# Windowed attention on one core: rotated queries and keys moved to whole heads, scores as products over 64 rows

## The reference, cut to what matters

```python
DEPTH, HEADS, DIM_HEAD, WINDOW = 6, 16, 64, 32      # x: (4, 512, 128)
q, k, v = (heads of x @ Wqkv)
q, k = l2norm(q) * qs, l2norm(k) * ksc
q = q * cos * scale + rotate_half(q) * sin * scale  # rotate_half: (-x2, x1)
k = k * cos / scale + rotate_half(k) * sin / scale
# each block of 32 queries sees its own 32 keys and the 32 before
attn = softmax(q_blk @ k_2blk.T * 8 where not masked)
x = x + (attn @ v_2blk) @ Wo, then x = x + gated FFN(layernorm(x))
```

## Time and profile before

| | |
|---|---|
| median of 3 runs | 2510.15 us (2502.93 to 2514.1) |
| the profiled execution | span 2515.4 us; no other time stands with it |
| instructions | 122,084, of them 53,677 MATMUL and as many LDWEIGHTS |
| transformer stage | from about 120 to 1845 us |
| DMA | 204.62 MB, mean 81 GB/s |

### The profile page before, as it was taken

How to read it: one execution, slowest core, us unless ns; L and a number is a source line. 1 busy time by engine, 2 the same in 40 slices (tenths; PEclk the granted TensorE clock), 3 DMA queues, 4 the chain that set the end, 5 groups by cost and what they waited for, 6 DMA issues and landing times.

```text
span 2515.4 us, 122084 instructions
## 1 busy us (share of the span) xinstructions
PE 2362.9 (94%) x53677; PEld 1738.9 (69%) x53677; DVE 1744.7 (69%) x3537; ACT 1598.6 (64%) x5036; POOL 1463.1 (58%) x1408
## 2 busy tenths in 40 slices
PE   9958999999999999999999999999878999999967
PEld 8836777777777777777777777777645666666657
DVE  4477888888878888878787888887335555555534
ACT  3226777777777787777777877777625444545422
POOL 1166667656666667666666677665117656566307
PEclk9979999999999999999999999999979999999978
DMA  4013333333333334333333343333216222222136
GB/s 91 15 33 86 85 78 96 95 80 85 93 88 94 81 83 103 92 83 81 88 95 85 79 97 82 84 92 84 57 22 185 48 48 48 48 48 48 30 95 250
DMA packets 230210, 204.62 MB, mean 81 GB/s; under 512 B 133687, under 2 KB 155464, under 8 KB 229552
## 3 DMA queue, kind: packets, MB, share of 16 engines
q1 hardware_dynamic: 225296, 190.91, 30.6%
q0 software_dynamic: 2208, 5.58, 0.6%
q10 hardware_dynamic: 2176, 0.33, 0.1%
HBM read 86.05 MB, written 15.70 MB: 40 GB/s over the span
## 4 chain that ended last, share of the span: by engine, by line
PE 72%; DVE 17%; issue 4%; SPq 2%; ACT 2%; DMA 1%; POOL 1%; POOLq 0%; ACTq 0%; DVEq 0%
PE psum L1208 8%; PE psum L1226 6%; PE psum L1955 5%; PE psum L1234 5%; PE psum L1109 5%; PE psum L1934 5%; PE psum L1940 4%; PE psum L1111 4%; PE psum L1110 3%; DVE kT L1443 3%; PE psum L1989 3%; PE psum L1979 3%; DVE rotated L1418 3%; PE psum L1185 2%; PE psum L1216 2%
## 5 line engine op out<-in xcount | busy, mean ns | idle before, releaser
L1354 ACT ACTIVATE p<-p,stat 128x64 f32<-128x64 f32 x1536 | 512.5, 336 | 40.1 <-DVE stat L1490 38.0
L1573 POOL TENSOR_TENSOR p<-p,inverse 128x512 f32<-128x512 f32 x192 | 200.2, 1043 | 465.9 <-DVE inverse L1493 464.9
L1208 PE MATMUL psum<-kT,qT 32*32 32x64 f32 x24576 | 306.7, 223 | 30.3 <-issue 29.1
L2088 DVE TENSOR_REDUCE largest<-psum 128x1 f32<-128x512 f32 x256 | 165.0, 686 | 228.0 <-PE psum L1940 228.0
L1208 PEld LDWEIGHTS psum<-kT,qT 32*32 32x32 f32 x24576 | 264.0, 103 | 82.2 <-issue 81.1
L1354 ACT ACTIVATION_READ_ACCUMULATOR p<-p,stat 128x1 f32 x1536 | 288.6, 188 | 0.0
L1418 DVE SCALAR_TENSOR_TENSOR rotated<-psum,scales,rotary 128x512 f32<-128x512 f32 x384 | 271.1, 742 | 24.3 <-ACT sq L1290 24.2
L1552 POOL TENSOR_TENSOR sq<-sq 128x512 f32<-128x512 f32 x192 | 245.1, 1276 | 42.4 <-ACT sq L1290 42.1
L1290 ACT ACTIVATE sq<-psum 128x512 f32<-128x512 f32 x384 | 212.8, 581 | 63.3 <-PE psum L1139 45.9
L1226 PEld LDWEIGHTS psum<-pT,v_win 64*64 64x64 f32 x12288 | 197.3, 135 | 47.6 <-issue 40.6
L1109 PE MATMUL psum<-xs,wqkv_high 128*128 128x512 f32 x384 | 204.9, 534 | 24.3 <-DVE rotated L1418 24.3
(11 more groups left out here) (352 smaller groups left out, 5448.6 us busy)
## 6 DMA issues: line engine op xcount, KB each, us to landing
v_win<-v_tok SPq DMA_DIRECT2D x576, 128.0 KB
rnorm_wide<-rnorms SPq DMA_DIRECT2D x384, 64.0 KB
v_win<-v_tok SPq DMA_DIRECT2D x336, 64.0 KB
q_rows<-q_rows_all SPq DMA_DIRECT2D x32, 512.0 KB, 4.6
tile_weights<-expert_table SPq DMA_DIRECT2D x23, 512.0 KB, 6.1
wqkv<-L_ffn_Wqkv SPq DMA_DIRECT2D x96, 64.0 KB, 2.4
rel_values<-sq SPq DMA_DIRECT2D x60, 64.0 KB, 2.2
wo<-L_ffn_Wo SPq DMA_DIRECT2D x48, 64.0 KB
```

Of the source, the lines that this page charges most:

```text
L1208: last = PE.e.matmul(psum[WIN * blk:WIN * (blk + 1), f, out], q[rows, g, half, tok:tok + WIN], k[rows, g, half, tok:tok + 2 * WIN], start= ...
L1354: last = A.e.activation(p, p, ACT.Exp, bias=t.stat[:, h, 2 * g + f:2 * g + f + 1], accum_out=t.sum[:, h, g, f:f + 1])
L1573: G.e.tensor_tensor(p, p, t.inv[:, h, :, :].unsqueeze(3).to_broadcast([P, GROUPS_TF, 2, 2 * WIN]), ALU.mult).then_inc(*t.p_scaled.by(m))
```

## The change

Each rotated half is written to one of three stage buffers. When GpSimd has finished it, SP moves it with two DMAs (`relay`): heads now lie whole in 64 partitions (`[half::2]`: the halves' features interleaved, in the same manner for queries and keys), two heads side by side. A score is then one product over 64 rows. A part's even and odd heads go to slots that change places for blocks 2 and 3 (`swapped`), odd heads' values are projected from tokens with each tile's 64-token halves exchanged (`x_swapped`, by ScalarE and GpSimd), and so ScalarE's copy of the values already is the window of the odd blocks; DMAs make that of the even ones alone. The mixing reads its two halves of 64 queries from two places. Norms are spread by 2 DMAs a group instead of 4. Several steps change rounds.

```diff
-VALUE_FIRST, WINDOWS_AT = 29, 31
+VALUE_FIRST, WINDOWS_AT, SWAP_AT = 33, 37, 28
-SQUARES_LAG, SUM_LAG, MADE_LAG = 2, 4, 3
-NORM_AT = {"root0": 17, "out": 15, "root1": 33, "turn": 39, "copy": 39}
-SPREAD_AT = (16, 18, 19, 24)
-SCALE_AT = (24, 28, 29, 32)
+SQUARES_LAG, SUM_LAG, MADE_LAG, RELAY_LAG = 2, 4, 3, 4
+NORM_AT = {"root0": 17, "out": 19, "root1": 33, "turn": 39, "copy": 39}
+SPREAD_AT = (20, 21, 25, 28)
+SCALE_AT = (24, 27, 28, 32)
+STAGES = 3
-SPLIT_AT = {2: 13, 3: 31, 0: 39, 1: 40, 4: 56, 5: 59}
+SPLIT_AT = {2: 13, 3: 31, 0: 39, 1: 40, 4: 60, 5: 62}
...
+def swapped(f, blk):
+    return f if blk < TPB // 2 else 1 - f
...
 def norms_wide(c, t, u, g):
...
-    for j in range(4):
-        src = bass.AP(t.rn_dram[u % 2].tensor, (j * GROUPS_TF + g) * S, [[0, HALF_D], [1, S]])
-        SP.e.dma_start(t.wide[g % 2][HALF_D * j:HALF_D * (j + 1), :], src).then_inc(*t.wide_in[g % 2].by((u, g, j)))
+    for e in range(2):
+        src = bass.AP(t.rn_dram[u % 2].tensor, (2 * e * GROUPS_TF + g) * S, [[GROUPS_TF * S, 2], [0, DH], [1, S]])
+        SP.e.dma_start(t.wide[g % 2][:, e, :], src).then_inc(*t.wide_in[g % 2].by((u, g, e)))
...
+def relay(c, t, u, p, half):
+    SP, k, (kind, g, lo) = c.SP, staged(u, p, half), piece(p)
+    SP.wait_ge(*t.made.on((u, (p, half))))
+    if u >= 2:
+        SP.wait_ge(*t.scored.on((u - 1) * PARTS - 1))
+    for e in range(2):
+        to = t.q[u % 2][half::2, g, e, :] if kind else t.k[u % 2][half::2, g, e, WIN:WIN + S]
+        SP.e.dma_start(to, t.stage[k % STAGES][e * H64:(e + 1) * H64, :]).then_inc(*t.relayed[k % STAGES].by((k, e)))
...
 def value_windows(c, t, n):
...
+    SP.e.dma_start(v[WIN:P, 1, 0, :, :], v[0:P - WIN, 0, 0, :, :]).then_inc(*v_in.by((n, 0)))
+    SP.e.dma_start(v[w1, 1, 1, :, :], v[w0, 0, 1, :, :]).then_inc(*v_in.by((n, 1)))
+    SP.e.dma_start(v[w0, 1, 1, :, :], v[w3, 0, 1, :, :]).then_inc(*v_in.by((n, 2)))
+    SP.e.dma_start(v[w3, 1, 1, :, :], v[w2, 0, 1, :, :]).then_inc(*v_in.by((n, 3)))
+    if n % TPB:
+        SP.e.dma_start(v[w0, 1, 0, :, :], before[w3, 0, 0, :, :]).then_inc(*v_in.by((n, 4)))
+        SP.e.dma_start(v[w2, 1, 1, :, :], before[w1, 0, 1, :, :]).then_inc(*v_in.by((n, 5)))
...
 def part_tensor(c, t, m, s):
...
-            for half in range(2):
-                for blk in range(TPB):
-                    tok, out = i * P + blk * WIN, slice(g * 2 * WIN, (g + 1) * 2 * WIN)
-                    for f in range(2):
-                        j = 2 * h + f
-                        rows = slice(HALF_D * j, HALF_D * (j + 1))
-                        last = PE.e.matmul(psum[WIN * blk:WIN * (blk + 1), f, out], q[rows, g, half, tok:tok + WIN], k[rows, g, half, tok:tok + 2 * WIN],
-                                           start=False, stop=(half == 1 and g == GROUPS_TF - 1))
+            for blk in range(TPB):
+                tok, out = i * P + blk * WIN, slice(g * 2 * WIN, (g + 1) * 2 * WIN)
+                for f in range(2):
+                    rows = slice(DH * f, DH * (f + 1))
+                    last = PE.e.matmul(psum[WIN * blk:WIN * (blk + 1), swapped(f, blk), out], q[rows, g, h, tok:tok + WIN], k[rows, g, h, tok:tok + 2 * WIN],
+                                       start=False, stop=(g == GROUPS_TF - 1))
...
-                        rows, to, at = slice(DH * f, DH * f + DH), (f + o) % 2 * DH, a * P + blk * WIN
-                        last = PE.e.matmul(psum[to:to + DH, 2 + o, at:at + WIN], v[rows, blk, 2 * (2 * a + o) + h, :],
+                        slot, to, at = swapped(f, blk), (f + o) % 2 * DH, a * P + blk * WIN
+                        rows = slice(DH * slot, DH * slot + DH)
+                        last = PE.e.matmul(psum[to:to + DH, 2 + swapped(o, blk), at:at + WIN], v[rows, 1 - blk % 2, f, 2 * (2 * a + o) + h, :],
...
-            last = PE.e.matmul(ps[:, 0:P], t.wo[:, e, :], t.ot[e % 2][:, e // 2, :], start=(e == 0), stop=(e == PAIRS - 1))
+            last = PE.e.matmul(ps[:, 0:P].rearrange("p (x q) -> p x q", x=2), t.wo[:, e, :], mixed_rows(t, e % 2, e // 2), start=(e == 0), stop=(e == PAIRS - 1))
...
+    if s == SWAP_AT:
+        if u:
+            A.wait_ge(*t.valued.on((u * TPB - 1, 1)))
+        for to, x in swap_halves(t, u, 0):
+            last = A.e.activation(to, x, ACT.Copy)
+        last.then_inc(*t.swap_high.by(u))
...
-        for m in (n - 2, n - 1):
-            if m >= 0:
-                A.wait_ge(*t.v_in[m % 2].on((m, 9 if m % TPB else 7)))
-        A.e.activation(t.vt[n % 2][:, f, :, 0:DH], ring_bank(c, t, "unit", u, f"v{i}{f}").rearrange("p (h d) -> p h d", d=DH), ACT.Copy).then_inc(*t.v_kept.by((n, f)))
+        if n >= 2:
+            A.wait_ge(*t.weighted.on(2 * (n - 2) + 1))
+        if n >= 1:
+            A.wait_ge(*t.v_in[(n - 1) % 2].on((n - 1, 5 if (n - 1) % TPB else 3)))
+        A.e.activation(t.v[n % 2][:, 0, f, :, :], ring_bank(c, t, "unit", u, f"v{i}{f}").rearrange("p (h d) -> p h d", d=DH), ACT.Copy).then_inc(*t.v_kept.by((n, f)))
...
 def unit_vector(c, t, u, s):
...
-        if u >= 2:
-            V.wait_ge(*t.scored.on((u - 1) * PARTS - 1))
+            if staged(u, p, half) >= STAGES:
+                V.wait_ge(*relayed_on(t, staged(u, p, half) - STAGES))
```

More of the change, by code:

```diff
@@ L750, in piece, with staged, relayed_on @@
     return kind, g, (1 - kind) * INNER + g * 4 * DH
-def made_of(t, u, kind, g):
-    return [t.q[u % 2][:, g, half, :] if kind else t.k[u % 2][:, g, half, WIN:WIN + S] for half in range(2)]
+def staged(u, p, half):
+    return (2 * GROUPS_TF * u + p) * 2 + half
+def relayed_on(t, k):
+    return t.relayed[k % STAGES].on((k, 1))
+def swapped(f, blk):
+    return f if blk < TPB // 2 else 1 - f
 def transformer_early_setup(c, scope):
@@ L790, in transformer_setup @@
     t.xs = [[sb(f"xs{i}_{k}", [P, S], F32R) for k in range(2)] for i in range(2)]
+    t.xp = [sb(f"x_swapped{k}", [P, S], F32R) for k in range(2)]
     t.xf = sb("x_ffn", [P, S])
@@ L794, in transformer_setup @@
     t.turned_by = [sb(f"rotated{i}", [P, S]) for i in range(2)]
[L795 to L796 removed]
+    t.stage = [sb(f"stage{i}", [P, S]) for i in range(STAGES)]
+    t.wide = [sb(f"rnorm_wide{i}", [P, 2, S]) for i in range(2)]
+    t.norms, t.rn, t.rn_t = [sb(f"norms{i}", [P, P]) for i in range(2)], [sb(f"rnorm{i}", [P, P]) for i in range(2)], t.wide[0][:, 0, 0:P]
     t.rn_dram = [nc.dram_tensor(f"rnorms{i}", (32, S), F32, kind="Internal").ap() for i in range(2)]
@@ L939, in transformer_sync @@
                 norms_wide(c, t, u, SPREAD_AT.index(s))
+            p, at = divmod(s - RELAY_LAG, 4)
+            if 0 <= p < 2 * GROUPS_TF and at == 0:
+                for half in range(2):
+                    relay(c, t, u, p, half)
             i, at = divmod(s - WINDOWS_AT, TILE)
@@ L1194, in part_tensor @@
         PE.wait_ge(*t.k_scaled.on((u, GROUPS_TF - 1)))
-        PE.wait_ge(*t.made.on((u, 2 * GROUPS_TF - 1)))
+        for back in range(STAGES):
+            PE.wait_ge(*relayed_on(t, staged(u + 1, 0, 0) - 1 - back))
         if m:
@@ L1262, in transformer_scalar, with swap_halves @@
                 unit_scalar(c, t, n, s)
+def swap_halves(t, u, k):
+    to, x = (y[:, :].rearrange("p (i a q) -> p i a q", i=TPB, a=2) for y in (t.xp[k], t.xs[u % 2][k]))
+    return [(to[:, :, 1 - a, :], x[:, :, a, :]) for a in range(2)]
 def shift_scalar(c, t, u):
@@ L1294, in unit_scalar @@
             A.wait_ge(*t.scores_kept.on((u - 1) * PARTS - 1))
-        A.e.activation(t.rq[u % 2][:, :, :].rearrange("p b r -> p (b r)"), ring_bank(c, t, "unit", u, "rn")[:, 0:P], ACT.Copy).then_inc(*t.rn_kept.by(u))
+        norms = ring_bank(c, t, "unit", u, "rn")[:, 0:P]
+        A.e.activation(t.rq[u % 2][0:H64, :, :].rearrange("p b r -> p (b r)"), norms[0:H64, :], ACT.Copy)
+        pairs = lambda x: x.rearrange("p (b a h f g) -> p b a h f g", b=TPB, a=2, h=2, f=2)
+        for f in range(2):
+            last = A.e.activation(pairs(t.rq[u % 2][H64:P, :, :].rearrange("p b r -> p (b r)"))[:, :, 1, :, 1 - f, :], pairs(norms[H64:P, :])[:, :, 1, :, f, :], ACT.Copy)
+        last.then_inc(*t.rn_kept.by(u))
     i, at = divmod(s - VALUE_FIRST - 1, TILE)
@@ L1440, in unit_vector @@
         k = t.k[u % 2][:, g, :, WIN:WIN + S]
-        V.wait_ge(*t.wide_in[g % 2].on((u, g, 3)))
-        V.wait_ge(*t.made.on((u, g)))
-        V.e.tensor_tensor(k, k, t.wide[g % 2][:, :].unsqueeze(1).to_broadcast([P, 2, S]), ALU.mult).then_inc(*t.k_scaled.by((u, g)))
+        V.wait_ge(*t.wide_in[g % 2].on((u, g, 1)))
+        for half in range(2):
+            V.wait_ge(*relayed_on(t, staged(u, g, half)))
+        V.e.tensor_tensor(k, k, t.wide[g % 2][:, :, :], ALU.mult).then_inc(*t.k_scaled.by((u, g)))
     feed_vector(c, t, u, s)
@@ L1548, in unit_gpsimd @@
         shift_gpsimd(c, t, u)
+    if s == SWAP_AT:
+        if u:
+            G.wait_ge(*t.valued.on((u * TPB - 1, 1)))
+        for to, x in swap_halves(t, u, 1):
+            last = G.e.tensor_copy(to, x)
+        last.then_inc(*t.swap_low.by(u))
     p, at = divmod(s - SQUARES_LAG, 4)
@@ L1556, in unit_gpsimd @@
```

(6 more changed lines are left out.)

48 lines of the change are left out of this document (22 added, 26 removed).

## The result

| | before | after |
|---|---|---|
| median | 2509.15 us (4 runs, 2502.93 to 2514.1) | 3207.3 us (4 runs, 3202.12 to 3211.68) |
| ratio | 1 | **1.2762** [1.2735, 1.2788] |
| span of the profiled execution | 2515.4 | 3200.3 |
| TensorE busy | 2362.9 | 2392.0 |

The change costs 698 us where 80 were to be gained. First the page: busy time and instructions of each engine; the chain's shares by engine and by line (cut); groups; DMA issues.

The account below looks back on a forecast made before the run. TensorE was taken to set the pace, VectorE close behind. Scores -100, stalls -20, VectorE taking over +30 and relays +7 gave -83: 2510 to 2427, rounded 2430 us; range 2375 to 2520.

Parts of the forecast that it names:

- Relays: Stage-buffer DMAs: one 0.3 us wait a unit before VectorE's third rotation of a piece, +7 us.
- Rival 2: Slower: VectorE's third rotation waits for stage buffers because SP issues relays late behind window DMAs; 2595 us, chance 13%.
- Later rounds: Value products four rounds later; a unit's first waits 0.9 us for ScalarE's third gate copy; taken as 0, bound +22 us.
- Scores: Score products over 64 rows: 64 MATMULs a part, 0.70 us instead of 1.41; -100 us after halving the chain's 8%.
- Stalls: TensorE's unnamed issue waits at the score products (29.1 and 81.1 us) partly go with fewer instructions; -20 us.
- VectorE takes over: Around the inverse roots VectorE is the chain, so TensorE's saving there becomes waiting; 1.3 us a unit given back, +30 us.
- Swaps and copies: Token swaps and small copies on ScalarE (1.3 us a unit) and GpSimd (up to 2) hide behind TensorE; 0.
- Rival 4: Score products over 64 rows save nothing, a part stays at 1.4 us from bank conflicts or drain; 2525 us, chance 6%.
- bank rule: Different row tiles can't access one PSUM bank at once; with swapped score slots, the sum would lose its first term.

Follow-up runs that it names:

- two_spreads: Changed kernel with each of a group's two spread DMAs filling 64 partitions, 64 repeats outermost and both rows inside; 2654.79 us, ratio 1.0486 to the kernel before.
- before_half_scores: Kernel before without its second-half score products (64 MATMULs of 32 rows a part), nothing else changed; 2491.59 us, ratio 0.9866.

## Why the prediction was wrong

3207 us lies far outside 2375 to 2520. By its steps:

- **Relays, +7: the step that failed.** Its place was right (the wait for the stage buffer before VectorE's third rotation). The slack of 3.7 us was too small if anything (6.0 and 6.6 in the two instances above). Its price took 2.4 us for the landing and held of the DMA engines, from their mean share, that "on their own they bind nothing". The mean stayed at 0.37, but a spread with an outermost count of 2 sits on two engines, and a relay behind it on the same queue lands when those two are through: 8.9 us in the median, with 28 of its 32 updates there after 2.5 us. I priced the spread by the old one, "with twice the bytes in all", though its form was new. Measured: 22.8 points for the form, 3.8 for the wait that is left.
- **Rival 2** named the wait and gave 2595 from SP's lateness. In two_spreads (2655) that is what happens, at 96 us of the 168 that it gave: SP 2.4 us late behind the spread, not behind window transfers, and 4.1 us of landing. In the changed kernel most query relays landed late, and SP was late in places: in the median it came to the relays within 0.03 us for 12 of a unit's 16 halves, but 4.7 and 8.4 us late for the two of piece 6, behind two groups of spreads. One instance, for a half that GpSimd finished at 1053.14:

```profile
1043.49 14.65 SPq L974 DMA_DIRECT2D rnorm_wide<-rnorms  x4
1058.19 5.39 SPq L987 DMA_DIRECT2D qT<-stage  x1
```

- **Later rounds, 0 with a bound of +22.** Wrong: +3.4%, some 85 us. I costed one copy of 0.9 us, not what else the moved steps hold up. Which of them carries the cost stays open.
- **Scores, -100: mis-sized.** A part took 0.79 us (said: 0.70; 0.62 us saved, not 0.71), so 119 us of TensorE went, not 136 (its busy time fell by 96 us in before_half_scores, 2362.9 to 2266.8). The larger error is the share that counts: 34 us of it and of the stalls together, where I had 100 + 20 - 30. The chain's 8% for L1208 was taken as time that would go. It says who ended last, not by how much, and here the second loop was 0 to 2 us a piece behind.
- **Stalls, -20.** Waits before L1208's successor fell from 29.1 + 81.1 to 49.0 us, even below the "under 70" foretold. They are part of the 34.
- **VectorE takes over, +30.** Right in kind, in before_half_scores its share of the chain is 34% (said: 25 to 30), too small in size: VectorE takes over together with ScalarE's exponentials, and in the short pieces too, not only beside the roots.
- **Swaps and copies, 0.** ScalarE's took 407 ns each, as said. GpSimd's two took 0.74 us together in the changed kernel and 1.74 in two_spreads (medians). No cost was seen or isolated.
- **Rival 4 and the bank rule.** The Trainium skill (TensorEngine Tiling (Array Packing), Gotcha 1: PSUM Pressure) has it that different row tiles can't access one PSUM bank at a time; a part took 0.79 us with the banks shared and with them apart. Not seen here.

In ratios (from separate comparisons, the first two of them made in the kernel before) the account nearly closes: halved scores -1.3, later rounds +3.4, stage wait +3.8, form of the spreads +22.8 make 28.7 of 27.6 points; the last -1.1 wasn't isolated. No version that computes the whole and keeps the relays beat the kernel before.

## What to carry to other kernels

Price a DMA by its form before its bytes: look at the outermost count of both access patterns, and when one is small, ask what stands behind it on the same engines and the same queue; a low mean share of 16 engines says nothing of two. Before counting a chain's share as gain, write down the next loop that closes over several engines and its period (here 7.35 us from four rotations, scaling, maxima, eight exponentials and a square on two engines), or take the work out of the kernel and time it: that run would have shown 1.3% at most. A moved step in a hand-written order is a cost of its own; run the new order alone first.
